# ViT tower with a top-2 mixture of experts: a first pair of its own, an own chunk and own output banks for the last rows, and GpSimd writing seven closing chunks

## What is computed

```
q, k, v = h @ Wq, split(h @ Wkv)                # 16 heads of 64, each image attends within itself
sim     = q k^T / 8;  P = reversed cumsum(sigmoid(sim)), cut to 63
sim    += lerp((q @ pos_emb)[floor P], (q @ pos_emb)[ceil P])
h       = layernorm(h + softmax(sim) v @ Wout + b_out)
s       = softmax(h @ router_w); the 2 best of 8 experts, weights s
routed  = sum over the 2: (silu(h Wg_e) * (h Wu_e)) Wd_e * s_e
shared  = (silu(h Sg) * (h Su)) Sd
out     = layernorm(h + shared + routed)
```

## Time and profile before

| | before |
|---|---|
| median of three runs | 785.13 us |
| the profiled execution | 790.15 us, span 788.4 us |
| TensorE busy | 735.7 us (93%) |
| VectorE busy | 511.1 us (65%) |
| ScalarE busy | 421.1 us (53%) |
| GpSimd busy | 160.1 us (20%) |

### The profile page before, as it was taken

How to read it: one execution, slowest core, us unless ns; L and a number is a source line. 1 busy time by engine, 2 the same in 40 slices (tenths; PEclk the granted TensorE clock), 3 DMA queues, 4 the chain that set the end, 5 groups by cost and what they waited for, 6 DMA issues and landing times. The chain is left out here.

```text
span 788.4 us, 14517 instructions
## 1 busy us (share of the span) xinstructions
PE 735.7 (93%) x5019; PEld 638.3 (81%) x5020; DVE 511.1 (65%) x1063; ACT 421.1 (53%) x780; POOL 160.1 (20%) x200
## 2 busy tenths in 40 slices
PE   5988999999999999999999979986999999999972
PEld 5867697979798897979797957775888999999862
DVE  0059898989798898989898988962442222222383
ACT  2365847565756758475656556321112555555264
POOL 2000000000000000000000000027532577776232
PEclk9999999999999999999999999988799999999997
DMA  8930001010102010010000033002001222221351
GB/s 294 315 117 17 19 24 45 23 45 23 45 0 65 3 41 27 23 34 23 12 23 12 6 119 113 23 15 25 1 2 31 66 78 83 87 83 55 141 172 71
DMA packets 28304, 47.36 MB, mean 60 GB/s; under 512 B 4794, under 2 KB 19108, under 8 KB 28275
## 3 DMA queue, kind: packets, MB, share of 16 engines
q1 hardware_dynamic: 22802, 37.24, 15.1%
q0 software_dynamic: 5472, 9.76, 4.0%
HBM read 35.57 MB, written 13.24 MB: 62 GB/s over the span
## 5 line engine op out<-in xcount | busy, mean ns | idle before, releaser
L584 POOL TENSOR_TENSOR rs<-ve,neg_half 111x2 f32<-111x2 f32 x11 | 12.5, 1133 | 472.6 <-DVE ve L1509 472.6
L758 PE MATMUL ps_X<-wkv_sb,hT 128*111 128x512 f32 (+1 forms) x176 | 85.7, 619 | 8.0 <-ACT v_sb L1150 7.5
L1034 PE MATMUL ps_S<-attnT,v_sb 128*128 128x128 f32 x704 | 85.9, 275 | 0.1
L1428 DVE COPY_PREDICATED table<-bit,table 111x112 f32<-111x112 int16 (+6 forms) x110 | 76.3, 694 | 11.4 <-DVE table L1428 0.2
L1034 PEld LDWEIGHTS ps_S<-attnT,v_sb 128*128 128x128 f32 x704 | 82.1, 192 | 0.3 <-issue 0.3
L1101 ACT COPY simS<-ps_S 32x666 f32<-32x666 f32 (+3 forms) x105 | 74.1, 705 | 13.4 <-DVE table L1485 10.5
L1758 DVE COPY attnT<-ps_S 128x256 f32<-128x256 f32 x44 | 18.7, 425 | 89.7 <-PE ps_S L1048 89.6
L758 PEld LDWEIGHTS ps_X<-wkv_sb,hT 128*111 128x111 f32 (+1 forms) x176 | 27.9, 174 | 50.7 <-issue 30.2
L699 PE MATMUL ps_S<-hT,wq_sb 128*128 128x222 f32 (+1 forms) x352 | 66.2, 345 | 0.0
L699 PEld LDWEIGHTS ps_S<-hT,wq_sb 128*128 128x128 f32 x352 | 63.5, 189 | 0.1
L794 PE MATMUL ps_X<-oT,wout_sb 128*128 128x222 f32 x320 | 61.9, 350 | 0.0
(11 more groups left out here) (212 smaller groups left out, 1383.5 us busy)
## 6 DMA issues: line engine op xcount, KB each, us to landing
down_sb<-in_x_dram SPq DMA_DIRECT2D x10, 648.0 KB
gu_sb<-y_d SPq DMA_DIRECT2D x8, 512.0 KB, 8.2
h_d<-hT SPq DMA_DIRECT2D x11, 222.0 KB, 2.7
kept<-h_d SPq DMA_DIRECT2D x11, 222.0 KB, 2.6
h_d<-h SPq DMA_DIRECT2D x10, 222.0 KB
wkv_sb<-in_L_attn_Wkv_dram SPq DMA_DIRECT2D x2, 1024.0 KB, 9.8
gu_sb<-in_L_ffn_gate_w_dram SPq DMA_DIRECT2D x2, 1024.0 KB, 11.2
gu_sb<-in_L_ffn_up_w_dram SPq DMA_DIRECT2D x2, 1024.0 KB, 12.3
```

The source lines that it names most:

```text
L758: mm = nc.tensor.matmul(X[:r, 1 - s], hT[:, k].rearrange("p b t -> p (b t)")[:, a * ROWS:a * ROWS + r], wkv_sb[:, k, INNER + 512 * s:INNER ...
L1034: mm = nc.tensor.matmul(S[:, i, j * FF + f * P:j * FF + f * P + P], held[:, i, k, j, f * P:f * P + P], xgT[:, i, k], start=(k == 0), stop= ...
L1428: A.did(V.copy_predicated(near[:, :, :, 0:SL - d], by_side(bit[:, n], r)[:, :, :, 0:SL - d], near[:, :, :, d:SL]))
```

## The change

**First pair.** SyncE issues the images first and the token weights in three parts; the small tables are issued by ScalarE. GpSimd and VectorE regroup half of pair 0 each. TensorE multiplies four fillers of 512 columns (`warm_up`), turns patches and token weights, and embeds in three parts; VectorE, not ScalarE, moves the turned weights. `first_pair` projects keys and queries by group (111 columns), group 0 first, and puts `queries(1)` ahead of the turned weights of group 0. The loop begins with pair 2.

**Own chunk.** The rows of the last pair (111 and 37) are chunk 9, `NEW`, and are read from `h1` in SBUF; chunk 8 has 86 and 86 rows. Chunks 7 and 8 are turned and routed at the end of the last pair, and batch 0 has 18 of 20 columns of rows. A mask `valid` replaces a memset. VectorE takes `residual` and `norm1` of pair 9 earlier. Some fillers go, others come. Before the tiles the gate products take three banks in turn. GpSimd scatters 40 times.

**Closing.** Each of the last chunks has output banks of its own (`out_banks`), rows are taken from the step after the first on, and GpSimd's `tensor_scalar` writes the normalised rows of the first seven chunks of `ORDER`.

The diff, cut to its core:

```
...
     CHUNK = PER * P
-    chunks = [(row, P, PER) for row in range(0, REAL - CHUNK + 1, CHUNK)]
-    chunks.append((REAL - REAL % CHUNK, REAL % CHUNK, 1))
+    DONE = (G2 - 1) * COLS
+    chunks = [(row, (P, P)) for row in range(0, DONE - CHUNK + 1, CHUNK)]
+    chunks.append((DONE - DONE % CHUNK, (DONE % CHUNK // PER,) * PER))
+    chunks.append((DONE, (ROWS, LAST * TOK)))
...
+        def rec(c, n):
+            if c == NEW:
+                return h1[:parts_of(c, n), n]
+            return rec_places[c][:parts_of(c, n), n * EMB:(n + 1) * EMB]
+
+        def both(c):
...
+        def bank_of(c, f):
+
+            if AT[c] < BEFORE:
+                return (S[:, 0], S[:, 1], X[:, 1])[(AT[c] * FC + f) % 3]
+            return S[:, f % 2]
+
+        def out_banks(c):
+
+            if AT[c] == BEFORE - 1 or AT[c] == BEFORE + 1:
+                return E
+            return X if AT[c] == BEFORE + 2 else S[:, 2:4]
...
-            sp.dma_start(w_nat[:, :, :], tok_w.rearrange("(t p) d -> p t d", p=P)).then_inc(w_tok, 16)
             load_x(0, XR)
-            sp.dma_start(pe_nat[:TOK, :], pos_embed[0]).then_inc(w_small, 16)
...
-                sp.dma_start(cope_nat[DH * h:DH * h + DH, :], cope_emb).then_inc(w_small, 16)
+            for s in range(3):
+                cols = slice(2 * s * P, 2 * s * P + 2 * P)
+                sp.dma_start(w_nat[:, :, cols], tok_w.rearrange("(t p) d -> p t d", p=P)[:, :, cols]).then_inc(w_tok[s], 16)
...
+            nc.gpsimd.tensor_copy(xp_sb[:, :NPH // 2, :].rearrange("p r (i w) -> p r i w", w=PATCH),
+                                  x_halves[:, :NPH // 2]).then_inc(xp_ready, 1)
...
+                if AT[c] < BY_POOL:
+                    pool.wait_ge(shift_ready, AT[c] + 1)
+                    for n in range(PER):
+                        rows = parts_of(c, n)
+                        mm = nc.gpsimd.tensor_scalar(y_of(c, 0, n), rec(c, n), rsc2[:rows, c, n:n + 1],
+                                                     shift2[:rows, c, n:n + 1], ALU.mult, ALU.add)
+                    mm.then_inc(out_pool, 1)
...
+            def by_group(bank, w, s, a):
+
+                for i in range(2):
+                    c = (2 * s + i) * P
+                    for k in range(KE):
+                        mm = nc.tensor.matmul(bank[:, i * ROWS:(i + 1) * ROWS], w[:, k, c:c + P],
+                                              hT[:, k, a * TPG:(a + 1) * TPG], start=(k == 0), stop=(k == KE - 1))
+                return mm
...
+                    pe.wait_ge(ot_sb, 2 * G - 2)
+                elif c == FULL + 1:
                     pe.wait_ge(h1_ready, 2 * G2)
-                elif c == FULL + 1:
-                    pe.wait_ge(rlg_ready, 1)
                 else:
-                    pe.wait_ge(h1t_sb, c - 1)
+                    pe.wait_ge(h1_ready, 2 * G2 + 2)
+                    pe.wait_ge(h1t_sb, c)
...
+            def first_pair():
+
+                pe.wait_ge(hT_ready, KE)
+                pe.wait_ge(w_k, 16)
+                for s in range(4):
+                    by_group(KA_BANKS[s], wkv_sb, s, 0).then_inc(ka_done, 1)
+                pe.wait_ge(w_q, 16)
+                for s in range(4):
+                    by_group(QA_BANKS[s], wq_sb, s, 0).then_inc(qa_done, 1)
+                pe.wait_ge(tables, N_TABLES)
+                score(0, 0)
+                for s in range(2):
+                    values(0, 0, s)
+                pe.wait_ge(sim_sb, 2)
+                pe.wait_ge(table_sb, 1)
+                for s in range(4):
+                    by_group(KB_BANKS[s], wkv_sb, s, 1).then_inc(k_done, 1)
+                values(0, 1, 0)
+                patches(1)
+                for s in range(4):
+                    if s < 3:
+                        pe.wait_ge(k_sb, s + 2)
+                    else:
+                        pe.wait_ge(xt_sb, 4)
+                    by_group(QB_BANKS[s], wq_sb, s, 1).then_inc(q_done, 1)
+                values(0, 1, 1)
+                score(0, 1)
+                pe.wait_ge(v_ready, 4)
+                pe.wait_ge(w_o, 16)
+                embed(1)
+                keys(1)
+                queries(1, True)
+                pe.wait_ge(q_sb, 4 + 2)
+                turn_weights(0, True)
+                pe.wait_ge(q_sb, 4 + 4)
+                outputs(0, 0)
+                patches(2)
 
             def pair(p, ahead, ahead2):
 
-                queries(p, ahead)
+                if next_first(p):
+                    pe.wait_ge(xt_sb, p * 3 + 6)
+                else:
+                    queries(p, ahead)
                 score(p, 0)
                 for s in range(2):
                     values(p, 0, s)
                 values(p, 1, 0)
-                if not first(p):
-                    turn_weights(p * 2 - 1, True)
...
                         route(c)
                         if c % 2 == 0:
                             shared_part(0, c // 4, c // 2 % 2)
-                        elif c < FULL - 1:
-                            warm(1, S[:, 2])
-
...
+            def warm_up(n):
+
+                for _ in range(n):
+                    nc.tensor.matmul(S[:, 2], ones[:, :], gate[:].rearrange("p h t -> p (h t)")[:, :512],
+                                     start=True, stop=True)
...
+            pe.wait_ge(zeroed, 1)
+            warm_up(4)
+            pe.wait_ge(consts, N_CONSTS)
+            pe.wait_ge(xp_other, 1)
+            patches(0)
+            turn_tok(0)
+            turn_tok(1)
+            pe.wait_ge(xt_sb, 3)
+            embed_part(0)
+            turn_tok(2)
+            embed_part(1)
+            pe.wait_ge(w_small, 64)
...
-            with pe.Fori(1, G2 - 2) as p:
+            embed_part(2)
+            first_pair()
+            pair(1, True, True)
...
                 if c == 0:
                     pe.wait_ge(h1_ready, 2 * G2 + 2)
-                else:
+                elif AT[c] < BEFORE - 1:
                     pe.wait_ge(sh_rec, AT[c])
-                for n in range(per):
+                elif AT[c] == BEFORE - 1:
+                    pe.wait_ge(ids_ready, 2)
+                elif AT[c] == BEFORE:
+                    pe.wait_ge(sh_rec, BEFORE - 1)
+                elif AT[c] == BEFORE + 1:
+                    pe.wait_ge(tile_y_sb, NT)
...
@@ -980,34 +1152,32 @@
                 pe.wait_ge(lists_num, 1)
                 nc.tensor.transpose(E[:, 1, :NT], lists_f[:NT, :], ident[:NT, :NT]).then_inc(lists_t, 1)
 
-            warm(2, S[:, 2])
+            warm(512)
+            warm(512)
             turn_weights(G - 1, False)
+            warm(256)
             outputs(G - 1, 1)
+            warm(256)
             pe.wait_ge(ot_sb, 2 * G)
             residual_half(G2 - 1, S[:, 2], 0)
             rank(0, 0, FIRST)
             residual_half(G2 - 1, S[:, 2], 1).then_inc(res_done, 1)
-            turn(FULL)
             shared_hidden(0, 2, 3)
             by_tokens(G2 - 1, S[:, 3])
-            route(FULL)
             shared_hidden(0, 3, 4)
             shared_hidden(1)
+            turn(NEW)
             shared_out(0)
-            turn(FULL + 1)
-            turn(FULL + 2)
-            shared_hidden(2, 0, 1)
-            route(FULL + 1)
...
             transpose_x(2, 0, 2)
             gate_up_tile(1, 1)
+            pe.wait_ge(sh_rec, BEFORE)
...
+                values(0, 1, 0)
+                patches(1)
+                for s in range(4):
+                    act.wait_ge(q_done, s + 1)
+                    nc.scalar.copy(qT[:, 2 * s:2 * s + 2, ROWS:], of_group(QB_BANKS[s])).then_inc(q_sb, 1)
+                regroup(2)
+                values(0, 1, 1)
+                for step in range(2):
+                    score(0, 1, step)
+                tables_out(0, 1)
+                gates(0, 1)
+                softmax_exp(0)
+                for s in range(4):
+                    keys(1, s)
+                for s in range(4):
...
-                    softmax_exp(p * 2 - 1)
+                if not next_first(p):
+                    for s in range(2, 4):
+                        queries(p, s)
...
-            act.wait_ge(setup_t, 3)
-            for s in range(3):
-                nc.scalar.copy(tokT[:, 2 * s:2 * s + 2], S[:, (2, 4, 5)[s]].rearrange("p (j e) -> p j e", j=2)
-                               ).then_inc(setup_sb, 1)
+                if not ahead:
+                    for c in range(FULL, NEW):
+                        turn(c)
+
+            act.dma_start(pe_nat[:TOK, :], pos_embed[0]).then_inc(w_small, 16)
+            act.dma_start(pe_nat[TOK:TOK + 1, :], tok_b.rearrange("(a e) -> a e", a=1)).then_inc(w_small, 16)
+            act.dma_start(pe_nat[TOK + 1:TOK + 2, :], cls_token[0]).then_inc(w_small, 16)
+            act.dma_start(pe_nat[TOK + 2:, :], b_out.rearrange("(a e) -> a e", a=1)).then_inc(w_small, 16)
...
+                if first(g):
+                    dve.wait_ge(sim_sb, 2)
...
                         embed(p + 1)
+                if not ahead:
+                    residual(p - 1, X[:, 1])
```

(22 more changed lines are left out.)

480 lines of the change are left out of this document (281 added, 199 removed).

## The result

The changed kernel takes 779.07 us in the median of 12 executions (774.66 to 783.93), the kernel before 786.07 beside it (783.99 to 790.14). The ratio is 0.9917, with a 95% interval of 0.989 to 0.9944: faster by 0.8%, or 7.0 us, where 17.8 were forecast. 779.07 lies above the range, which ended at 775.5. Its executions sort by their granted clock: 774.66, 775.19 and 775.21 have a mean of 0.976, 783.78 and 783.93 one of 0.961.

A forecast was written before the change was run, and what follows sets the result against it. TensorE, nearly always busy in the pair loop, was taken to lose time outside it, with VectorE limiting the closing. Opening -6.0, junction -8.9 and closing -2.9 sum to -17.8: median 785.1 becomes 767.3 us, range 760 to 775.5.

The forecast's parts named there:

- Opening, -6.0: Start of kernel through first pair: earlier first keys (4.5 us) and a rearranged first pair (1.5) gain 6.0 us.
- rival B: Opening: warm-up ends late, clock still low for the embedding; opening gives only -1.5, total 771.8 us; chance 0.10.
- Rank 0, +3.4: Junction: rank of batch 0 comes 2.4 us later at full clock, 5 at half; +3.4 taken.
- rival A: Junction: clock falls in TensorE's new wait at 507, lists later; junction gives -4.5, total 771.7 us; chance 0.13.
- Rank 0 to the lists, -13.7: Junction, from batch 0's rank to the turned lists: 66.5 us replaces 80.2, GpSimd's scatters setting the end.
- Closing and own chunk, -1.5: After the lists: wider own chunk costs +1.4 us, closing stage with own output banks gains 2.9.
- my bound of 0.9: Closing stage: GpSimd's 14 half-chunk writes stay hidden as long as one costs under 0.9 us.
- rival D: Closing stage: GpSimd becomes the bound; gain used up at 2.2 us a write, about 790 at 2.5; chance 0.03.
- The allowance for port waits, 0.9 us: Closing stage: VectorE waiting out GpSimd's writes on the shared port costs 0.9 us, bounds 0 and 6.3.
- Rival C: Closing stage: VectorE waits 0.4 us for each GpSimd write; closing +3.0, total 773.2 us; chance 0.09.

The follow-up runs named there:

- sets 1 and 3: Two rounds of follow-up runs, engines pausing: kernel before 813.11 and 813.93 us, changed kernel unaltered 819.88 and 819.32 us (ratios 1.0078 and 1.0061).
- sets 1 and 2: Two rounds of follow-up runs, each with the unaltered kernel before: 813.11 us in the one with pauses, 784.18 us in the one without.

## Why the prediction failed, step by step

Three steps failed: the filler products were counted as time and not as what holds the clock; the gain behind rank 0 was taken from one slow execution of before; and GpSimd's writes were called hidden by a mean over the stretch.

**Opening, -6.0: right, too small by about one.** Up to the first keys it is -5.2 (17.54 for 22.74), forecast -4.5. The scores of group 2 come at 69.1 to 69.7 for 76.0 to 77.3, and the opening alone measured -6.9 and -7.8. The pace that rival B doubted was there: the twelve patch transposes take 1.30 us for 2.42, the first eight instructions of the embedding 1.75 us, 0.22 each for 0.30. B falls. The granted clock reads 1.00 for the first 25 us of both kernels, so the low clock that the prediction assumes there stands in no record; and no run leaves the warm-up products out, so that they did it is argued, not shown.

**Rank 0, +3.4: the mechanism failed, and the number held in the short executions by luck.** It said "TensorE, rid of three filler products (2.9 us), is there at 507 and waits 2 us", and counted the fillers as time. They held the clock: before has 1.00 through its routings, the changed kernel and its variants without them fall to 0.50 at 491 to 497 in every profile (at 500 to 503 with the opening of before, where all is 7 us later), and with the fillers back it does not before 504. From the scores of group 2 to rank 0 before needs 442.0 and 441.9 us. The three kernels with fillers and four chunks need 444.9 to 445.0, the changed kernel 445.5 with 10 us of low clock, 450.3 with 24 (the one with four chunks by GpSimd), 454.2 with 31: +3.0, +3.5, +8.4, +12.3. The short low clock costs little, since it covers TensorE's wait for the rows of chunk 8 (1.87 us in the kernel that holds the clock). I had an upper end of +5 for "all at half clock", from the wrong place: I looked for the low clock only behind a wait (rival A), and it came without one. A had the right kind and the wrong trigger; its 771.7 was still too low.

**Rank 0 to the lists, -13.7: right for one execution.** The changed kernel needs 67.4 us in both undisturbed profiles, forecast 66.5, with GpSimd's cast released last as written. What was wrong is what it was taken from. The 80.2 us of the first profile held 14.4 us of low clock behind the load; the second profile of before has 3.9 there and needs 74.5. The step is therefore between -7.1 and -12.8. The prediction also said: "I assume that this difference stays", of the 5.0 us by which the profiled execution was above the median. It lay for the most part (5.7 us between the two profiles) in a stretch that the change removes, so it could not stay.

**Closing and own chunk, -1.5: two errors.** From the lists to VectorE's end before needs 179.4 and 180.2 us, the changed kernel 179.2 and 178.8, forecast 177.9. The kernels in which GpSimd writes four chunks need 177.9, 177.9 and 178.3, the one in which ScalarE writes all 179.6. So four chunks by GpSimd gain 1.2 to 1.6 us here, and with seven most of it is gone, with 2.4 lost behind VectorE's last row. From the lists to the end of the span it is 187.4 to 187.9 with four chunks, 190.7 to 191.5 in five profiles with seven, 189.1 with none, and 189.0 and 189.7 before: with four the forecast of -1.5 would have held. The write was estimated at 0.45 us and takes 0.72. The groups of VectorE's and GpSimd's row operations in the changed kernel (busy, mean ns), and GpSimd's first operation for the second chunk:

```profile
L2019 DVE SCALAR_TENSOR_TENSOR wkv_sb<-gu_sb,top,wkv_sb 128x256 f32<-128x256 f32 x16 | 8.5, 532 | 0.6
L2017 DVE SCALAR_TENSOR_TENSOR wkv_sb<-gu_sb,top,wkv_sb 128x256 f32<-128x256 f32 x16 | 8.0, 503 | 0.0
L745 POOL TENSOR_SCALAR gu_sb<-wkv_sb,rsc,shift 128x256 f32<-128x256 f32 x12 | 8.6, 724 | 0.6
...
742.65 0.19 POOL L733 TENSOR_SCALAR vec<-resT 128x2 f32<-128x2 f32 x1 [3.15 <-ACT gu_sb L1543]
```

0.72 is below my bound of 0.9, and yet GpSimd is late by 2.4 us. The bound was wrong: it divided the free time of the whole stretch by 14 writes, as if GpSimd could use the time ahead of the first chunk. VectorE finishes a chunk every 2.7 us (the second at 739.11, the seventh at 752.41), and GpSimd needs 3.1 for each (742.65 to 757.94 for five). So it starts the seventh 5.4 us behind VectorE: 3.4 were there at the second, for which it had waited for ScalarE's squares, and 2.0 grew since. That is rival D, at 0.72 us a write and not at 2.2, and with a price of 2.4.

The allowance for port waits, 0.9 us, was about right. VectorE's two row operations grow from 0.487 and 0.480 us (the same groups of before) to 0.532 and 0.503, 1.1 us over 32; all 40 take 20.9 us for 19.3 where ScalarE writes, 1.6 us. The Trainium skill (SBUF — State Buffer, section "SBUF: two separate sides") has GpSimd and such VectorE operations shut each other out for a whole instruction; 10.1 us of writes beside VectorE cost it 1.6, so this trace shows far less than a full lock. Rival C, 0.4 us a write, falls at 0.11. (Its own sum was off: 14 x 0.4 - 3.8 is +1.8, not +3.0, and gives 772.0.)

**The sum.** The change was forecast at -17.8 us and measured -7.0. Between the two profiled executions, on which the terms were made, the four steps are -7.8, +3.5, -12.8 and, from the lists to the end of the span, +2.2 (191.15 for 188.95), where -6.0, +3.4, -13.7 and -1.5 were forecast: -14.9, which is 2.9 short, by the closing stage. The other 7.9 us of the miss come from taking these two executions for the medians. That of before lies 4.1 us above its median of 786.07; that the low clock behind the load makes it slow is shown by the second profile. That of the changed kernel lies 3.9 below its median of 779.07; that the median has more low clock in the routings rests on the mean clocks (0.970 to 0.972 for 0.976) and on the price that the profiles with 24 and 31 us give, for none was had of a median execution.

## What to carry to other kernels

Products that nobody reads may be what keeps the clock: before they are counted as time saved, look at the granted clock of the stretch and ask what dense work is left there, and place them between thin products, not ahead of the chain that decides. When the profiled execution is slower than the median, find the stretch that makes it so before subtracting anything from that stretch. Whether an engine off the path is hidden is decided by its pace against the one that feeds it, chunk by chunk, and not by its mean over the stretch.

## What was not expected

**The clock falls in a busy stretch, for very different times.** With TensorE busy in 14.85 of 16 us, the clock falls in the stretch of products of 8 columns and stays at 0.50 for 10 to 31 us in executions of the same kernel, 9 us of run time apart. The Trainium skill (TensorE: Matmul & The Clock Gate, Part 1) says that the transition at the start of a kernel varies from run to run; here the way back in mid-kernel does, by 20 us. Why it is short or long is open.

**Engines that stop with nothing to wait for.** In sets 1 and 3 before took 28 us more and the changed kernel 41; sets 1 and 2 ran on the same chip, so it is not the chip alone. Up to 450 us the traces agree. Then, in the changed kernel, ScalarE, TensorE and VectorE pause between 540 and 582 us, while GpSimd's scatters go on at their usual pace. TensorE's and VectorE's timelines of set 3:

```profile
550.20 0.40 PE L1126 MATMUL ps_S<-simS,earlier_than 128*128 128x16 f32 x2 [3.05 <-issue]
...
572.76 0.59 PE L1146 MATMUL ps_S<-sdown_sb,v_sb 128*128 128x256 f32 x1 [2.21 <-issue]
575.56 0.59 PE L1146 MATMUL ps_S<-sdown_sb,v_sb 128*128 128x256 f32 x1 [2.21 <-issue]
578.36 0.58 PE L1146 MATMUL ps_S<-sdown_sb,v_sb 128*128 128x256 f32 x1 [2.22 <-issue]
581.16 2.21 PE L1146 MATMUL ps_S<-sdown_sb,v_sb 128*128 128x256 f32 x4 [2.21 <-issue]
```

```profile
557.16 0.42 DVE L1889 SCALAR_TENSOR_TENSOR nb<-ex,ps_X 128x256 f32<-128x256 f32 x1 [7.01 <-issue]
...
577.39 0.42 DVE L1889 SCALAR_TENSOR_TENSOR nb<-ex,ps_S 128x256 f32<-128x256 f32 x1 [19.35 <-issue]
```

Sixteen instructions that take 3.6 us elsewhere take 22 here, seven of them behind a pause for which no releaser is found, and VectorE stands for 19 us.

The lists come 91.5 us behind rank 0 and not 67.4, and from the lists to VectorE's end every kernel takes 13 to 15 us more. The kernel with the new opening alone needs 89.6 us for the same step in set 1, so the junction's gain is gone there and its costs remain: the change is 0.7% slower than before in both sets. TensorE's instructions start 2.1 or 2.8 us apart. I read this as instructions that arrive late, since the code of the junction is written out; against it, the tile loop is slower too. The Trainium skill (Runtime: NRT & Kernel Launch, section "Instruction fetch mechanics") says that this supply is mostly hidden; the profiles of the other sets agree, and if my reading is right these do not. The cause was not shown: the run that held back the scatters fell into a calm set.
